# GNN stack on one core: the weight pass splits 42 of 50 columns into bf16 parts instead of 24, ScalarE weighs every column, and the splitting moves to VectorE

## The reference, cut to what matters

```
h   = relu(layernorm(x))
agg = segment_sum(h[src] * edge_weight[:, None], dst, num_segments=6250)
x   = x + agg @ W.T + b
```

## Time and profile before

| | us |
|---|---|
| median of 3 runs | 4877.57 (4873.73 to 4878.07) |
| the profiled execution's own time | 4874.45 |
| its span in the profile | 4872.6 |
| weight pass, from DVE's first copy (line 2288) to the instruction behind its last eviction (line 2455) | 2459.27 to 3135.96 |
| one block of the weight pass, from a gather of 30 matmuls to the next block's | 13.62 |
| one block of the count pass | 9.24 |

### The profile page before, as it was taken

One profiled execution on the slowest core, in us unless ns is written; L12 is line 12 of the kernel. 1 busy time (PEld: TensorE's weight loads), 2 busy tenths in 40 slices (PEclk: granted clock), 3 DMA queues, 4 the chain that ended last, 5 costly groups with the idle time before them and its releaser, 6 DMA issues.

```text
span 4872.6 us, 255836 instructions
## 1 busy us (share of the span) xinstructions
PE 4363.9 (90%) x102320; PEld 3919.5 (80%) x102320; DVE 4086.2 (84%) x6303; ACT 2785.9 (57%) x9065; POOL 965.3 (20%) x1099
## 2 busy tenths in 40 slices
PE   1899999749999995899889999889999998999998
PEld 1677777549999995788779999868888887888887
DVE  7799999979999999888888888977777667776776
ACT  1999999612222222777733333466666666666665
POOL 2355555423333332000022222100000000000000
PEclk7999999969999998999989999999999999999999
DMA  1000000048888983000044444343333333333333
GB/s 54 2 1 1 2 1 2 17 144 285 285 285 284 284 284 132 14 0 0 0 113 120 120 119 121 82 110 96 97 98 97 96 95 97 99 100 97 100 101 81
DMA packets 305221, 501.39 MB, mean 103 GB/s; under 512 B 76918, under 2 KB 78454, under 8 KB 305126
## 3 DMA queue, kind: packets, MB, share of 16 engines
q1 hardware_dynamic: 303782, 499.39, 34.9%
q0 software_dynamic: 576, 0.52, 0.1%
q10 hardware_dynamic: 768, 0.16, 0.0%
HBM read 408.40 MB, written 91.57 MB: 103 GB/s over the span
## 4 chain that ended last, share of the span: by engine, by line
PE 50%; issue 17%; DVE 15%; ACT 13%; POOL 3%; DMA 1%; DVEq 1%; ACTq 0%; POOLq 0%; SPq 0%
PE PS L1539 20%; ACT arena L874 12%; PE PS L1532 9%; PE PS L1312 5%; PE PS L1314 5%; DVE arena L1848 4%; PE PS L1336 4%; DVE arena L2484 4%; PE PS L1330 3%; POOL arena L803 3%; PE PS L1570 1%; PE PS L1468 1%; PE PS L1453 1%; PE PS L1343 1%; DVE arena L2410 1%
## 5 line engine op out<-in xcount | busy, mean ns | idle before, releaser
L1848 DVE TENSOR_TENSOR arena<-iotab,arena 128x1024 bf16<-128x1024 bf16 (+3 forms) x1887 | 1655.2, 911 | 228.3 <-PE PS L1539 168.7
L1063 ACT ACTIVATE arena<-PS 128x384 bf16<-128x384 f32 x2450 | 1001.5, 499 | 546.9 <-PE PS L1532 546.9
L1539 PE MATMUL PS<-arena 32*128 32x193 bf16 (+1 forms) x41552 | 995.3, 242 | 46.6 <-DVEq L2485 42.6
L1539 PEld LDWEIGHTS PS<-arena 32*128 32x128 bf16 x41552 | 838.5, 92 | 151.7 <-DVEq L2485 59.5
L874 ACT ACTIVATE arena<-PS,m 128x196 bf16<-128x196 f32 x1813 | 738.0, 446 | 21.8 <-PE PS L1171 21.7
L1532 PE MATMUL PS<-Hp,arena 128*128 128x192 bf16 (+1 forms) x4900 | 539.5, 248 | 35.0 <-DVE Hp L1692 34.5
L1312 PE MATMUL PS<-Hp,arena 128*128 128x72 bf16 x7350 | 501.6, 198 | 46.0 <-DVE arena L2194 40.4
L1314 PE MATMUL PS<-arena 128*128 128x72 bf16 x7350 | 502.1, 199 | 0.0
L1532 PEld LDWEIGHTS PS<-Hp,arena 128*128 128x128 bf16 x4900 | 381.1, 99 | 149.1 <-issue 83.5
L1043 ACT ACTIVATE arena<-PS,ewB 128x64 f32<-128x64 f32 x1176 | 256.6, 329 | 418.4 <-PE PS L1376 418.3
L1178 PE MATMUL PS<-arena,tmp 128*128 128x262 bf16 x1813 | 450.8, 277 | 17.1 <-DVE tmp L1848 14.2
(11 more groups left out here) (376 smaller groups left out, 8091.4 us busy)
## 6 DMA issues: line engine op xcount, KB each, us to landing
arena<-hots SPq DMA_DIRECT2D x735, 256.0 KB, 2.7
arena<-codes SPq DMA_DIRECT2D x245, 512.0 KB, 5.1
hots<-arena SPq DMA_DIRECT2D x245, 256.0 KB, 5.2
arena<-hots SPq DMA_DIRECT2D x147, 320.0 KB, 2.9
arena<-codes SPq DMA_DIRECT2D x49, 640.0 KB, 5.8
hots<-arena SPq DMA_DIRECT2D x49, 320.0 KB, 5.4
rows_h<-Hn SPq DMA_DIRECT2D x4, 1568.0 KB, 9.4
rows_l<-Y SPq DMA_DIRECT2D x1, 1764.0 KB, 9.8
```

The source lines that it names most:

```text
L1063: act.activation(RG[ROW_BUFFER[g]][:, 2 * i:2 * i + 2, 0:RW], ps[PAIR_BANK[q]][:, 0:2 * RW].rearrange("p (k c) -> p k c", k=2), ACT.Copy). ...
L1539: last = pe.matmul(ps[2 + q][:, b * SW:b * SW + SW - o], one_hot[32 * q:32 * q + 32, b * P:(b + 1) * P], rows_of[32 * q:32 * q + 32, 0:SW ...
L1848: return dve.tensor_tensor(to.rearrange("p k (n t) -> p k n t", t=4), iota_of[:, 0:n].rearrange("p (n t) -> p n t", t=4)[:, None, :, :] .t ...
```

## The change

All 50 columns of a block are weighed by ACT. Groups 0 to 4 (42 columns) are split into three bf16 parts and scattered in bf16, group 5 (8 columns) stays whole in float32; its rows are no longer multiplied by DVE. Both subtractions of the split run on DVE; POOL does nothing in the loop. Each group has its own W3q and one-hot buffer; gathered rows use three pairs of banks in turn, (0,1), (2,3), (5,7), sums use banks 4 and 6, and a block has two evictions. PE gathers three groups ahead of the scatter instead of one. The fourfold codes are written by ACT, a half block at a time (`own_codes`), the second half during the block itself. The evictions signal by the instruction's own semaphore increment and DVE doesn't wait for them; so does the count pass's eviction.

```diff
-        w_OD = [cv.take(GS[0] * P).rearrange("p (k n) -> p k n", n=P) for _ in range(3)]
-        w_OB = [cv.take(GS[1] * P, bf16).rearrange("p (k n) -> p k n", n=P) for _ in range(3)]
-        Wq = [cv.take(GS[0] * DIM).rearrange("p (k c) -> p k c", c=DIM) for _ in range(3)]
-        W3q = [cv.take(GS[1] * PARTS * DIM).rearrange("p (k a c) -> p k a c", a=PARTS, c=DIM) for _ in range(3)]
+        w_OB = [cv.take(n * P, bf16).rearrange("p (k n) -> p k n", n=P) for n in GS[0:NG - 1]] + \
+            [cv.take(GS[NG - 1] * P).rearrange("p (k n) -> p k n", n=P)]
+        W3q = [cv.take(n * PARTS * DIM).rearrange("p (k a c) -> p k a c", a=PARTS, c=DIM) for n in GS[0:NG - 1]] + \
+            [cv.take(GS[NG - 1] * DIM).rearrange("p (k a c) -> p k a c", a=1, c=DIM)]
...
-            a = 2 * (g % 2) + (k >= m)
-            return ps[a][:, (k % m) * WIDE:(k % m) * WIDE + WIDE]
+            a = ((0, 1), (2, 3), (5, 7))[g % 3][k // m]
+            return ps[a][:, (k % m) * DIM:(k % m + 1) * DIM]
+
+        def wait_weighed(engine, dx, g):
+            engine.wait_ge(b_whole, dx * NG + (g + 1))
...                                                   (POOL)
-                with pool.Fori(0, WINDOWS) as d:
-                    lowest_part(d, 0)
-                    lowest_part(d, 1)
-                    lowest_part(d, 2)
...                                                   (ACT)
+                def own_codes(dx, h):
+                    if not is_zero(dx):
+                        act.wait_ge(f_ohd, dx * NG + (2 * NN - 3 + 3 * h))
+                    cols = slice(0, HALF) if h == 0 else slice(HALF, CPW)
+                    act.activation(w_cdw[:, cols, :], ... fourfold ..., ACT.Copy).then_inc(f_codes, 1)
+
+                def weigh_rows(dx, last):
+                    for g in range(NG):
+                        act.wait_ge(f_gath, dx * NG + (2 * NN + g + 4))
+                        if not is_zero(dx):
+                            act.wait_ge(b_scat, dx * NG + (g + 1 - NG))
                         for k in range(GS[g]):
-                            last = act.activation(W3q[i][:, k, 0, :], bank_at(g, k)[:, 0:DIM], ACT.Copy,
-                                                  scale=ewB[:, bass.ds(d * CPW + (G0[g] + k), 1)])
+                            done = act.activation(W3q[g][:, k, 0, :], bank_at(g, k), ACT.Copy,
+                                                  scale=ewB[:, bass.ds(dx * CPW + (G0[g] + k), 1)])
+                        done.then_inc(b_whole, 1)
+                        if g == 1 and not is_zero(dx):
+                            own_codes(dx, 1)
+                        if g == 4 and not last:
+                            own_codes(dx + 1, 0)
...                                                   (PE)
+            def scatter_parts(dx, g):
+                h = g // 3
                 to = ps[4 + 2 * h][:, 0:DIM]
+                if g < NG - 1:
+                    pe.wait_ge(b_low, dx * (NG - 1) + (g + 1))
+                else:
+                    wait_weighed(pe, dx, g)
                 pe.wait_ge(f_ohd, dx * NG + (2 * NN + g + 1))
...
             def weigh_edges():
+                def body(dx, last):
+                    for g in range(NG):
+                        if g < NG - 3:
+                            gather_rows_at(dx, g + 3)
+                        elif not last:
+                            gather_rows_at(dx + 1, g + 3 - NG)
+                        scatter_parts(dx, g)
...                                                   (DVE)
+                def rest(dx, g):
+                    wait_weighed(dve, dx, g)
+                    dve.tensor_tensor(W3q[g][:, :, 1, :], W3q[g][:, :, 0, :], Wup[g][:, :, 0, :],
                                       ALU.subtract).then_inc(b_rest, 1)
+
+                def lowest_part(dx, g):
+                    dve.wait_ge(b_rest, dx * (NG - 1) + (g + 1))
+                    dve.tensor_tensor(W3q[g][:, :, 2, :], W3q[g][:, :, 1, :], Wup[g][:, :, 1, :],
+                                      ALU.subtract).then_inc(b_low, 1)
+
+                def operands(dx, g):
+                    if g < NG - 1:
+                        rest(dx, g)
+                    one_hots(dx, g)
+                    if g < NG - 1:
+                        lowest_part(dx, g)
...
-                    flink(dve.tensor_tensor(to, to, ps[4 + 2 * h][:, 0:DIM], ALU.add))
-                    dve.sem_inc(f_accout, 1)
+                    dve.tensor_tensor(to, to, ps[4 + 2 * h][:, 0:DIM], ALU.add).then_inc(f_accout, 1)
...
                 def body(dx, first, last):
+                    for g in range(NG):
+                        if not (last and g + 1 == NG):
+                            operands(dx + (g + 1) // NG, (g + 1) % NG)
+                        if g == 1 and not first:
                             evict(dx - 1, 1)
+                        if g == 2:
                             few(dx)
+                        if g == 4:
                             evict(dx, 0)
...                                                   (count pass, DVE)
-                    flink(dve.tensor_tensor(to, to, ps[6][:, 0:CV], ALU.add))
-                    dve.sem_inc(f_accout, 2)
+                    dve.tensor_tensor(to, to, ps[6][:, 0:CV], ALU.add).then_inc(f_accout, 2)
```

More of the change, by code:

```diff
@@ L1035, in _ @@
             with act.If(runs < 2):
[L1036 to L1041, removed]
-                        for k in range(GS[g]):
-                            last = act.activation(W3q[i][:, k, 0, :], bank_at(g, k)[:, 0:DIM], ACT.Copy,
-                                                  scale=ewB[:, bass.ds(d * CPW + (G0[g] + k), 1)])
-                        last.then_inc(b_whole, 1)
+                def own_codes(dx, h):
+                    if not is_zero(dx):
+                        act.wait_ge(f_ohd, dx * NG + (2 * NN - 3 + 3 * h))
+                    cols = slice(0, HALF) if h == 0 else slice(HALF, CPW)
+                    act.activation(w_cdw[:, cols, :], cdA3[:, bass.ds(dx, 1), cols].rearrange("p w c -> p (w c)")
+                                   [:, :, None].to_broadcast((P, cols.stop - cols.start, 4)), ACT.Copy).then_inc(f_codes, 1)
+                def weigh_rows(dx, last):
[3 more added lines that the diff above has]
+                            act.wait_ge(b_scat, dx * NG + (g + 1 - NG))
+                        for k in range(GS[g]):
+                            done = act.activation(W3q[g][:, k, 0, :], bank_at(g, k), ACT.Copy,
[5 more added lines that the diff above has]
+                            own_codes(dx + 1, 0)
+                own_codes(0, 0)
+                own_codes(0, 1)
+                weigh_rows(0, False)
+                with act.Fori(1, LASTW) as d:
+                    weigh_rows(d, False)
+                weigh_rows(LASTW, True)
             parts_of_h(4)
@@ L1359, in attend_edges, with gather_rows_at @@
                 body(LASTW, True)
-            def gather_rows_at(dx, i, whole):
-                g = 2 * i + (not whole)
+            def gather_rows_at(dx, g):
                 pe.wait_ge(f_hot[g], dx * 16 + 16)
[L1365 to L1368, removed]
+                if g >= 3:
+                    wait_weighed(pe, dx, g - 3)
+                elif not is_zero(dx):
+                    wait_weighed(pe, dx - 1, g + 3)
                 for k in range(GS[g]):
@@ L1398, in scatter_whole @@
                     last.then_inc(f_sum, 1)
[L1400 to L1412, removed]
-            def weigh_edges():
[L1415 to L1436, removed]
+            def weigh_edges():
+                def body(dx, last):
[5 more added lines that the diff above has]
+                        scatter_parts(dx, g)
+                for g in range(3):
+                    gather_rows_at(0, g)
+                with pe.Fori(0, LASTW) as d:
+                    body(d, False)
+                body(LASTW, True)
             pe.wait_ge(s_begin, 1)
@@ L2279, in attention_pass @@
                 dve.sem_inc(f_ohd, 4 * WINDOWS)
[L2281 to L2298, removed]
-                    dve.wait_ge(f_gath, dx * NG + (2 * NN + g + 4))
-                    w = ewB[:, bass.ds(dx * CPW + G0[g], GS[g])].rearrange("p (h k) -> p h k", h=2)
-                    rows_at = ps2(0, 2)[:, :, 0:m * WIDE].rearrange("p h (k c) -> p h k c", c=WIDE)[:, :, :, 0:DIM]
-                    dve.tensor_tensor(Wq[i][:, 0:GS[g], :].rearrange("p (h k) c -> p h k c", h=2), rows_at,
-                                      bc(w, DIM), ALU.mult).then_inc(f_whole, 1)
-                def ps2(a, n):
-                    return PS[:, a * 512:(a + n) * 512].rearrange("p (b x) -> p b x", b=n)
-                def rest(dx, i):
-                    dve.wait_ge(b_whole, dx * 3 + (i + 2))
-                    dve.tensor_tensor(W3q[i][:, :, 1, :], W3q[i][:, :, 0, :], Wup[i][:, :, 0, :],
-                                      ALU.subtract).then_inc(b_rest, 1)
@@ new lines, in weight_pass, with one_hots @@
+            def weight_pass():
```

(12 more changed lines are left out.)

72 lines of the change are left out of this document (23 added, 49 removed).

## The result

| | before | changed |
|---|---|---|
| median, us | 4876.49 (4873.73 to 4878.07, 4 runs) | 4747.56 (4744.27 to 4763.33, 4 runs) |
| ratio | | 0.9745 (95%: 0.9728 to 0.9763) |
| profiled execution / its span | 4874.45 / 4872.6 | 4763.33 / 4761.2 |
| attention pass, first to last score (DVE) | 851.8 | 860.2 |
| count pass, memset of Hp to reciprocal of st | 462.3 | 446.8 |

The changed kernel is 129 us faster, against 116 forecast (4762). The weight pass gave 111 us and the count pass 15.5. The profiled execution is 16 us slower than the median of its kernel, and that is not from the change: its attention pass, which is the same in both kernels, took 860 us. In the profiles of this study that pass takes either 843 to 845 us or 860 to 862 (852 once, before), in kernels that don't differ in it, so two kernels are best compared by the length of the pass in question.

The account below looks back on a forecast made before the run. PE and DVE were both taken as limits of the 13.62 us weight block; DVE's 11.3 plus 0.2 makes 11.5, gaining 104 us, plus 12 in the count pass: 4877.57 down to 4762, range 4740 to 4806.

Parts of the forecast that it names:

- PE after: Weight pass: PE needs 10.8 us a block with fewer float32 scatters, between 10.5 and 11.2.
- DVE after: Weight pass: DVE's distances between starts sum to 11.3 us a block, between 11.1 and 11.9.
- ACT after: Weight pass: ACT needs 10.9 us a block for 50 weighings and the codes, between 10.6 and 11.4.
- rival 1: Weight pass: ACT becomes the bound, 12.5 or 12.0 us a block, total 4811 or 4787 us; chance 0.17.
- case (b): Weight pass: ACT at step 0.202, bare group ends and waits needs 12.0 us a block, total 4787; chance 0.08.
- The ring: Weight pass: PE, DVE and ACT depend on each other in a cycle; 0.2 us a block added for it.
- rival 2: Weight pass: the three closely matched engines lose more than 0.2 us to each other, block 12.0, total 4786; chance 0.12.
- Fill and drain: Weight pass: the 9.3 us outside the blocks, at its start and end, stay within 3 us.
- Count pass: Count pass: removing the gap behind the eviction gains 10.6 to 14.5 us, taken as 12.
- Rival 3: Weight pass: ACT held at the codes' second half exposes weighings, block 15.0 us, total 4933, slower; chance 0.04.
- Rival 4: Count pass: the gap is the eviction's own latency and stays, 12 us less gain, 4774; inside the forecast's 0.60.
- Rival 5: Both passes: more gain, DVE at 11.1 us without waits and 14.5 in the count pass, total 4740; chance 0.07.

Follow-up runs that it names:

- six groups: Changed kernel with the sixth group split as well, all 50 columns: weight pass 28.3 us longer than the change's, median 4767.19 us.
- the count pass alone: Kernel before with only the count pass's eviction unlinked: count pass 447.7 us against 462.3, median 4857.96 us, ratio 0.9961.

## Why the prediction was right, point by point

- **Bounds before.** PE and DVE both at the limit: shown. Unlinking DVE's sums gained 17.6 of a possible 53 us and stopped at PE's 13.24.
- **PE after, 10.8.** 10.63 by the run without the last subtraction. The float32 column at 0.226 us and the split one at 0.088 are right: with one group more in float32 the block is at 11.72, where 11.73 was worked out.
- **DVE after, 11.3.** Exact: 11.30, and 11.97 for 11.96 with six groups. The reserve up to 11.9 for gaps behind the evictions was not needed; 0.14 each. Two signs of being right, lengths of 0.55 (few columns) and 0.68 us (subtractions), came out as 0.62 and 0.75: the rule "length less 0.08" doesn't hold in the changed kernel, the distances do. That gaps would have cost 0.6 a block is shown by linking them (+30.4 us).
- **ACT after, 10.9.** Too high but not in the way: it does its 50 columns and the codes in 10.63 or less. The larger step of 240 ns, an estimate from the figures in the Trainium skill, ScalarE: Activation LUTs, section "What ACT_TABLE_LOAD costs", stood beside rival 1; it is refuted for this instruction by 0.197 in an unbroken row of 26. The bare group ends of case (b) did not show either, since that row runs over several groups.
- **The ring.** I added 0.2 us for three engines so close together, and it is the term that was furthest off: nothing was lost, in the steady blocks DVE has not one gap, and rival 2 with it is refuted. That is 10 us too little gain; the ends took 2.4 of it back, the count pass adds 3.5, and the 2 that are left of the 13 by which the forecast was too high are within the interval of the ratio (116 to 133 us). The argument for the slack (a group's way of 5.3 us against 7.6) fits that DVE never waits, and the reserve on top had no row behind it. Whether it takes all three groups of lookahead, or the third pair of banks, was not tested.
- **Fill and drain.** 49 x 2.32 is 113.7 us, 111.3 were gained: 2.4 lost at the ends, inside the 3 left for it.
- **Count pass, 12.** 14.6 to 15.5 measured, at or over the upper end of 14.5: 0.31 a block, not the 0.25 taken. The distance from the eviction to the next compare fell from 0.45 to 0.14, which could have been read off as 0.45 less the attention pass's unlinked distance (0.135 in the kernel before); I counted the gap and part of the overlap.
- **Rival 3 (code hand-over)** did not come up: DVE waits for ACT only while the pass fills, 8.1 us in five waits, and never between 2500 and 3000 us. **Rival 4** is refuted by the count pass alone. **Rival 5** (4740) is nearer to the measured 4747.6 than the forecast (4762): its "without any wait" and its count pass came true, its 11.1 for DVE did not.
- **The lock.** The prediction took POOL's share of the work over at 3.14 us and named only the 0.6 saved at the few columns; that the bf16 compares, too, had been held up (0.79 for 0.60) went in unsaid, by taking 0.60 for them. The runs show that the move is right: left on POOL, the five subtractions cost 61.5 us more.

No variant of the weight pass is shorter than the change's, except the one that leaves out the last part. Moving a few columns from the split groups to the float32 one would bring DVE (11.30) and PE (10.63) closer; it wasn't tried.

## What to carry to other kernels

Work out each engine's time as the sum of the distances between starts, not of the lengths, and take the largest; where buffers give a group's way clear slack (here 5.3 us in 7.6), adding nothing for the coupling was right. Before giving DVE's work to POOL, compare POOL's length with DVE's distance for the same thing, here 1.42 us with 0.60: where both read two SBUF inputs, they held each other up. On an engine at its limit, a wait for the own result costs the gap and the lost overlap, here 0.32 us (0.46 for 0.14).

## What the runs showed of the hardware that was not expected

- A DVE or ACT instruction can be recorded longer at the same distance: ACT's 329 and 484 ns both go with a step of 0.20 us; DVE's 0.68 and 0.75 with 0.60.
- The attention pass, unchanged in all these kernels, has two lengths, 843 to 845 and 860 to 862 us. In the longer one POOL's subtraction of 8 columns takes 1606 ns on average where it takes 1437 in the shorter, and PE waits for POOL 9 us in 800 where it waited for nothing. DVE's few columns' compare takes 1448 ns for 552, and its 128x2048 instruction 881 for 978: POOL holds up another DVE instruction than in the shorter one. What puts an execution into the one or the other stays open. The 852 us of the kernel before are no third kind: the few columns' compare has 551 ns there, and the 8 us more are a single stumble in the first 100 us, where DVE is busy for 91.60 of 100 us and the granted clock is 0.94 on average, against 100 and 1.00 in the run with the count pass alone.
